# Small reductions over pairs of columns in place of small tensor_scalar operations, the floor of the scales moved into the maxima, and a new table of orders

## The chip, the core and the metric

The kernel runs on one core of one Trainium2 chip. A core has engines that each work through a queue of their own: TensorE (matmuls, which read SBUF and write PSUM), VectorE, ScalarE (both read and write SBUF and PSUM), GpSimd (SBUF only; POOL in the profile) and SyncE (SP), which here only issues DMA transfers. They wait for each other by semaphores. The metric is the device time of one execution in microseconds; lower is better.

## The reference, cut to what matters

A batch of 16 images (3 x 96 x 96) is cut into 36 patches of 16 x 16, each mapped to 256 features; a class token goes in front, 128 text tokens behind: 165 tokens of 256 features per image. On them one transformer layer works:

```python
h = concat([tok(x), txt], axis=1)                     # 16 x 165 x 256
h = h + attn(layernorm(h), Wq, Wk, Wv, Wo)            # 16 heads, 4 key heads, window |q-k| <= 32, rope, softmax
h = h + ffn(layernorm(h), w1, conv_w, conv_b, w2)

def act_quant(x):
    scale = 127.0 / clip(max(abs(x), axis=-1, keepdims=True), 1e-05)
    return clip(round(x * scale), -128, 127) / scale
def weight_quant(w):
    scale = 1.0 / clip(mean(abs(w)), 1e-05)
    return clip(round(w * scale), -1, 1) / scale
def ffn(x, w1, conv_w, conv_b, w2):                   # 256 -> 1024 -> 256
    g = act_quant(x) @ weight_quant(w1).T
    g = silu(depthwise_conv1d(g, conv_w, conv_b))     # three taps along the tokens
    return act_quant(g) @ weight_quant(w2).T
```

What the change touches is the variance of each layernorm (`var + eps`) and, in each `act_quant`, the scale of a token: `max(amax, 1e-05) / 127`, its reciprocal, and its product with the scale of the weights.

## The kernel before

The 16 images are worked in eight pairs (n = 0 to 7) of 330 tokens. A pair's tokens lie as 3 tiles of 110 partitions (t = 0 to 2); attention goes over 11 blocks (j) of 30 queries with a key window of up to 94, in 3 groups (k) of four, four and three blocks; the FFN goes over 8 slices (m) of 128 hidden features in two halves, for the last pair in four quarters. All pairs are in flight as in a pipeline: while the attention of pair n runs, the FFN of pair n-2 or n-1 is between its pieces.

Each piece of work is a small function on its engine that waits for its semaphores and issues its instructions. The order in which an engine takes them is written out by hand in the table ORDER (and ONCE for what happens once): a place in the engine's queue for each piece. Each engine walks the places upwards. An engine never goes past a piece that waits, so a place decides both when a piece may start and what it holds up.

The pieces that the change and the prediction's steps touch, by engine:

- VectorE, startup: sort_pix and keep_pix (L1293, L1298) arrange the pixels of the four image loads; stats1(n) (L1337, L1341, L1344) takes mean and variance of a pair's tokens, after the DMA that moves its patch tokens into `h`; abs_w (L1307, two of them) sums |w1| and |w2|, and ternary (L1314 to L1330) rounds the weights.
- VectorE, attention: max_s(n,j) (L1393) is the row maximum of the scores in PSUM; TensorE's shift(n,j) (L1760) waits for it. norm(n,k) (L1401, L1403) divides by the sums; add_att(n,t) (L1409, L1411) adds the output projection and takes statistics; var2(n) (L1418, L1421) makes the variance, of which GpSimd's rstd2 (L976) makes the power -0.5 and norm2 (L1027) the normalised `xn2` in SBUF.
- VectorE, scale of the FFN input: max_x(n) takes the largest |x| per token (L1428), the clipped scale (L1431), its reciprocal (L1433), for which ScalarE's quant_x (L1174) waits, and the product with the weight scale w1s (L1434), for which GpSimd's dequant_x (L1035) waits. low_x (L1441) splits the input for TensorE's up(n,m) (L1840, L1841).
- FFN: mid on ScalarE (L1190) and taps(n,m) on VectorE (L1449, L1452) make the convolution; tanh on ScalarE (L1198); silu on VectorE (L1458) or on GpSimd (L1043, L1045, two passes over 128 x 1320, both operands in SBUF); abs_g on ScalarE (L1206); max_g on VectorE (L1475, L1479, L1482; for the last pair L1468, L1473). scale_2(n) is max_x's counterpart (L1489, L1492, L1494, L1495); TensorE's spread (L1855) waits for its reciprocal. quant_g (L1502), ScalarE's conv_g (L1213), TensorE's down(n,t) (L1867) and add_ffn(n,t) (L1510) follow. store sends a pair out.
- The last pair's norm is cut by tiles and made on VectorE: var_last(t) (L1516, L1518), rstd_last(t) on GpSimd (L1049), norm_last(t) (L1523 to L1540, seven small or 110 x 256 operations), turn_last(t) on TensorE (L1874), high_last, low_last (L1546), then up(7,m).

Of the kernel before, what the change touches and what calls it, by code (L numbers as in the profile page):

```python
# [103 lines left out]
def tok_tiles(n):  # L104
# [28 lines left out]
        (182, 184),
        (246, 250),
        (328, 334),
        (395, 402),
    ),
    'pe.project': (
        (6, 7, 8),
        (24, 32, 42),  # L140
        (84, 87, 97),
        (136, 141, 147),
        (187, 190, 204),
        (252, 264, 268),
        (339, 343, 347),
        (411, 417, 424),
    ),
    'pe.turn_q': (
        (11, 12, 15),
        (46, 57, 66),  # L150
        (105, 116, 121),
        (154, 169, 174),
        (208, 225, 230),
        (287, 300, 312),
        (360, 371, 384),
        (447, 452, 460),
    ),
    'pe.turn_k': (
        (13, 14),
        (68, 73),  # L160
        (124, None),
        (179, None),
        (239, None),
        (322, None),
        (387, None),
        (485, None),
    ),
# [50 lines left out]
    'pe.select': (
        (49, 71, 90),
        (123, 142, 157),  # L220
        (193, 220, 241),
        (272, 293, 319),
        (344, 368, 389),
        (421, 457, 476),
        (496, 521, 536),
        (564, 589, 600),
    ),
# [1734 lines left out]
```

## Time and profile before

| | before |
|---|---|
| median of 3 runs | 401.66 us (400.25 to 404.05) |
| profiled execution | 399.73 us, of which the span 397.9 us |
| TensorE matmul busy | 343.9 us (86%), 2910 instructions |
| VectorE busy | 302.5 us (76%), 643 |
| ScalarE busy | 259.2 us (65%), 486 |
| GpSimd busy | 248.2 us (62%), 244 |
| chain that ended last | TensorE 49%, VectorE 20%, GpSimd 14%, issue 6%, DMA 5%, ScalarE 4% |
| granted TensorE clock, mean | 0.956 of full speed; lower only near 25 us and in the last 30 us |

The span is the time from the first to the last instruction. Busy shares are means over stages with different limits, so they do not say what bounds the kernel; the busy time by stretch and the waits within a stretch do. A group of instructions has one row with its count, its busy time in all and the mean duration of one. In a timeline, the bracket at the end of a row is the time that the engine stood idle before it, and what it had waited for. The chain that ended last is followed back from the last instruction, at each step to what released it.

### The profile page before, as it was taken

Reading aid. Unit: us, or ns where it says so; the run is one execution under the profiler, and the core shown is the slowest. Engines: PE = TensorE matmul, PEld = TensorE weight load, DVE = VectorE, ACT = ScalarE, POOL = GpSimd, SP = SyncE. Lnnn points to the kernel's source line nnn. Section 1 sums busy time; section 2 is a strip of 40 time slices with the busy share of each in tenths; the row PEclk is TensorE's granted clock in tenths of the full one; section 3 lists DMA queues with packets and bytes.
Section 4 is the critical chain, followed back from the end, with each engine's and each line's share of the span. In section 5 each row is a group of like instructions: output and inputs, shape, how many; then the busy total and the mean of one; then the engine's idle time right before and its main releaser. Section 6 shows DMA issues by size and latency. Waiting matters only on the chain.

```text
span 397.9 us, 8286 instructions
## 1 busy us (share of the span) xinstructions
PE 343.9 (86%) x2910; PEld 267.9 (67%) x2910; DVE 302.5 (76%) x643; ACT 259.2 (65%) x486; POOL 248.2 (62%) x244
## 2 busy tenths in 40 slices
PE   1579999999999989999999997989989989844564
PEld 1356666767787668867986796778857857634454
DVE  2164548744568889897889759998888899898984
ACT  3232554857767869867887767679777787534732
POOL 3407189299899994999489957991760563051510
PEclk9998999999999999999999999999999999995856
DMA  7772161000000100020001002000010210001001
GB/s 233 170 163 55 34 213 28 16 13 15 26 20 18 35 1 3 17 59 20 6 18 33 9 18 61 17 0 2 2 26 22 69 49 1 2 0 36 1 16 52
DMA packets 20250, 15.71 MB, mean 39 GB/s; under 512 B 11035, under 2 KB 19160, under 8 KB 20209
## 3 DMA queue, kind: packets, MB, share of 16 engines
q1 hardware_dynamic: 19314, 14.02, 13.7%
q10 hardware_dynamic: 895, 1.16, 1.1%
q8 instruction: 23, 0.38, 0.4%
q14 instruction: 18, 0.15, 0.1%
HBM read 7.91 MB, written 2.70 MB: 27 GB/s over the span
## 4 chain that ended last, share of the span: by engine, by line
PE 49%; DVE 20%; POOL 14%; issue 6%; DMA 5%; ACT 4%; SPq 1%; ACTq 0%; DVEq 0%; POOLq 0%
PE bank L1769 6%; PE bank L1840 4%; PE bank L1867 4%; PE bank L1784 3%; PE bank L1841 3%; POOL shared L1027 3%; PE bank L1741 3%; PE bank L1689 3%; PE bank L1760 3%; PE bank L1811 3%; DMA cst<-in_consts 3%; PE bank L1636 2%; POOL shared L1035 2%; PE bank L1752 2%; PE bank L1802 2%
## 5 line engine op out<-in xcount | busy, mean ns | idle before, releaser
L1393 DVE TENSOR_REDUCE mx<-bank 120x4 fp32r<-120x376 f32 (+3 forms) x88 | 44.5, 509 | 29.7 <-PE bank L1752 28.9
L1154 ACT COPY pT<-bank 94x480 f32<-94x480 f32 (+3 forms) x88 | 48.6, 555 | 15.4 <-PE bank L1769 14.9
L1145 ACT ACTIVATE pr<-bank 120x376 f32<-120x376 f32 (+3 forms) x88 | 39.9, 457 | 26.0 <-PE bank L1760 25.2
L1769 PE MATMUL bank<-cst,pr 120*94 120x120 f32 (+3 forms) x352 | 51.1, 269 | 3.2 <-ACT pr L1145 2.8
L1840 PE MATMUL bank<-xT_hi,w1T 128*128 128x330 f32 x128 | 45.6, 362 | 4.1 <-DVE wn L1452 2.4
L1769 PEld LDWEIGHTS bank<-cst,pr 120*94 120x94 f32 (+3 forms) x352 | 36.6, 121 | 12.5 <-ACT pr L1145 6.7
L1841 PE MATMUL bank<-xT_lo,w1T 128*128 128x330 f32 x128 | 41.1, 326 | 0.0
L1689 PE MATMUL bank<-wqk,xnT 128*110 128x384 f32 x96 | 36.8, 512 | 0.2
L1760 PE MATMUL bank<-mx,neg_id 120*120 120x376 f32 (+3 forms) x88 | 33.0, 386 | 4.0 <-DVE mx L1393 3.9
L1867 PE MATMUL bank<-w2T,shared 128*110 128x256 bf16 x192 | 29.2, 305 | 8.0 <-DVE h L1510 3.7
L1752 PE MATMUL bank<-kbd,q_hl 128*120 128x376 f32 (+3 forms) x88 | 36.1, 410 | 0.0
L1741 PE MATMUL bank<-kbd,q_hl 128*120 128x376 f32 (+3 forms) x88 | 35.6, 405 | 0.5 <-ACT pT L1154 0.4
L1043 POOL TENSOR_TENSOR shared<-shared,wn 128x1320 f32<-128x1320 f32 (+1 forms) x5 | 12.2, 2436 | 35.0 <-ACT shared L1198 35.0
L983 POOL TENSOR_SCALAR xn<-h,mv,rs 110x256 f32<-110x256 f32 x21 | 27.9, 1336 | 9.6 <-PE bank L1677 9.4
L1784 PE MATMUL bank<-pT,vw 94*32 94x120 f32 (+3 forms) x704 | 33.5, 286 | 0.2
L1867 PEld LDWEIGHTS bank<-w2T,shared 128*110 128x110 bf16 x192 | 24.6, 146 | 10.6 <-issue 5.3
L976 POOL TENSOR_TENSOR rs<-ve,half_neg 110x3 f32<-110x3 f32 x15 | 15.1, 1005 | 25.5 <-DVE ve L1344 18.9
L1027 POOL TENSOR_SCALAR shared<-h,mv,rs 110x256 f32<-110x256 f32 x21 | 30.2, 1449 | 1.1 <-POOL rs L976 1.1
L1840 PEld LDWEIGHTS bank<-xT_hi,w1T 128*128 128x128 f32 x128 | 25.5, 199 | 7.3 <-DVE wn L1452 3.2
L1035 POOL TENSOR_SCALAR shared<-shared,am 110x256 f32<-110x256 f32 x21 | 25.4, 1220 | 6.4 <-ACT shared L1174 6.4
L1005 POOL TENSOR_TENSOR qkr<-rc,rsn 110x160 f32<-110x160 f32 x44 | 26.8, 631 | 1.7
L1784 PEld LDWEIGHTS bank<-pT,vw 94*32 94x32 f32 (+3 forms) x704 | 18.8, 144 | 12.1 <-issue 8.2
(149 smaller groups left out, 918.4 us busy)
## 6 DMA issues: line engine op xcount, KB each, us to landing
out<-h SPq DMA_DIRECT2D x7, 330.0 KB
wn<-in_w SPq DMA_DIRECT2D x2, 1024.0 KB, 7.0
kbd<-kT SPq DMA_DIRECT2D x96, 20.6 KB, 1.9
shared<-in_x SPq DMA_DIRECT2D x4, 432.0 KB
h<-in_txt SPq DMA_DIRECT2D x1, 770.0 KB
wlT<-in_lin SPq DMA_DIRECT2D x1, 768.0 KB, 7.3
h<-tokp SPq DMA_DIRECT2D x14, 36.0 KB
h<-in_txt SPq DMA_DIRECT2D x1, 448.0 KB
```

The source lines that it names most:

```text
L1027: o = nc.gpsimd.tensor_scalar(xn2[:, t, :], h[:, n, t, :], mv2[:, t, 0:1], rs2[:, t:t + 1], ALU.subtract, ALU.mult)
L1154: nc.scalar.copy(pT[0:cnt, g % 3, :], S_BANKS[g % 2][0:cnt, 0:HKV * QP]).then_inc(p_kept, 1)
L1393: nc.vector.tensor_reduce(mx[:, g % 4, :].bitcast(F32R), S_BANKS[g % 2][0:QP, 0:HKV * KEYS[j][1]].rearrange("p (k c) -> p k c", k=HKV), ax ...
L1689: o = nc.tensor.matmul(qk_bank(n, t)[0:TT, 0:QKC + QK], xnT[:, k, t * TT:(t + 1) * TT], wqk[:, k, :], start=(k == 0), stop=(k == KD - 1))
L1741: nc.tensor.matmul(dst, q, kbd[n % 2][:, 0, :, k0:k0 + cnt].bitcast(F32R), start=True, stop=False)
L1752: o = nc.tensor.matmul(dst, q, kbd[n % 2][:, 1, :, k0:k0 + cnt].bitcast(F32R), start=False, stop=True)
L1760: nc.tensor.matmul(S_BANKS[g % 2][0:QP, 0:HKV * cnt], neg_id[:, :].bitcast(F32R), mx[:, g % 4, :].bitcast(F32R).unsqueeze(2).to_broadcast( ...
L1769: o = nc.tensor.transpose(S_BANKS[g % 2][0:cnt, kv * QP:(kv + 1) * QP], pr[:, g % 3, kv * cnt:(kv + 1) * cnt], ident[0:QP, 0:QP])
L1784: o = nc.tensor.matmul(C_BANK[VS * kv:VS * (kv + 1), col:col + QP], vw[n % 2][0:cnt, j, :, kv], pT[0:cnt, g % 3, kv * QP:(kv + 1) * QP], s ...
L1840: nc.tensor.matmul(dst, w, xT_hi[:, k, :].bitcast(F32R), start=(k == 0), stop=False)
L1841: o = nc.tensor.matmul(dst, w, xT_lo[:, k, :].bitcast(F32R), start=False, stop=(k == KD - 1))
L1867: o = nc.tensor.matmul(down_bank(n, t), gq[:, m, t * TT:(t + 1) * TT], w2T[:, m, :], start=(m == 0), stop=(m == MH - 1))
```

## The change

Small operations. In stats1 and var2 the addition of eps to three variances was a tensor_scalar; now the tile `mv` has a third column that holds eps, and a tensor_reduce adds the pair (variance, eps). In max_x and scale_2 a tensor_scalar took the maximum with the floor and multiplied by 1/127, and another multiplied by the weight scale; now new tiles `two1` and `two2` hold pairs (value, 1/127) and (scale, weight scale), and a tensor_reduce multiplies each pair. The floor went elsewhere: for the FFN input it is a 257th column of each row of `xn2` that the maximum takes in; for the hidden activations it is the scalar of a scalar_tensor_tensor that takes the place of the last tensor_tensor maximum of max_g. The constants are written by four VectorE memsets at its start and one GpSimd memset in norm2(0). The last pair's norm_last keeps its tensor_scalar operations; its var_last takes the new form. `xn2` now has rows of 257 columns, so `ga` behind it starts three columns later.

```diff
-        xn2, at = carve(shared, at, TT, [NT, D])
+        xn2, at = carve(shared, at, TT, [NT, D + 1])
...
-        mv1 = sb("mv1", [TT, NT, 2])
+        mv1 = sb("mv1", [TT, NT, 3])
...
+        two1 = sb("two1", [TT, 2, NT, 2])
+        two2 = sb("two2", [TT, 2, NT, 2])
...
+                if n == 0:
+                    nc.gpsimd.memset(xn2[:, :, D:D + 1], CLIP_MIN)
...
+            nc.vector.memset(two1[:, 0, :, 1:2], 1.0 / QMAX)
+            nc.vector.memset(two2[:, 0, :, 1:2], 1.0 / QMAX)
+            nc.vector.memset(mv1[:, :, 2:3], LN_EPS)
+            nc.vector.memset(mv2[:, :, 2:3], LN_EPS).then_inc(guards_made, 1)
...
-                    nc.vector.tensor_scalar(w2s[:, :], wstat[:, 1:2], 0.5, None, ALU.mult)
+                    nc.vector.tensor_scalar(two1[:, 1, :, 1], wstat[0:TT, 0:1].to_broadcast([TT, NT]), 1.0, None, ALU.mult)
+                    nc.vector.tensor_scalar(two2[:, 1, :, 1], wstat[0:TT, 1:2].to_broadcast([TT, NT]), 0.5, None, ALU.mult)
...
-                nc.vector.tensor_scalar(ve2[:, :], mv2[:, :, 1], LN_EPS, None, ALU.add).then_inc(var2, 1)
+                nc.vector.tensor_reduce(ve2[:, :], mv2[:, :, 1:3], axis=AX.X, op=ALU.add).then_inc(var2, 1)
...
-                nc.vector.tensor_reduce(am1[:, 0, :], xn2[:, :, :], axis=AX.X, op=ALU.max,
+                nc.vector.tensor_reduce(two1[:, 0, :, 0], xn2[:, :, :], axis=AX.X, op=ALU.max,
                                         apply_absolute_value=True).then_inc(max1, 1)
                 dve.wait_ge(max1, n + 1)
-                nc.vector.tensor_scalar(am1[:, 1, :], am1[:, 0, :], CLIP_MIN, 1.0 / QMAX, ALU.max, ALU.mult).then_inc(clip1, 1)
+                nc.vector.tensor_reduce(two1[:, 1, :, 0], two1[:, 0, :, :], axis=AX.X, op=ALU.mult).then_inc(clip1, 1)
                 dve.wait_ge(clip1, n + 1)
-                nc.vector.reciprocal(am1[:, 2, :], am1[:, 1, :]).then_inc(scale1, 1)
-                nc.vector.tensor_scalar(am1[:, 3, :], am1[:, 1, :], w1s[0:TT, 0:1], None, ALU.mult).then_inc(undo1, 1)
+                nc.vector.reciprocal(am1[:, 2, :], two1[:, 1, :, 0]).then_inc(scale1, 1)
+                nc.vector.tensor_reduce(am1[:, 3, :], two1[:, 1, :, :], axis=AX.X, op=ALU.mult).then_inc(undo1, 1)
...
-                    nc.vector.tensor_tensor(gm[:, 2, :], gm[:, 0, :], gm[:, 1, :], ALU.max).then_inc(g_maxed, 1)
+                    nc.vector.scalar_tensor_tensor(out=gm[:, 2, :], in0=gm[:, 0, :], scalar=2 * CLIP_MIN, in1=gm[:, 1, :],
+                                                   op0=ALU.max, op1=ALU.max).then_inc(g_maxed, 1)
...
```

stats1, scale_2 and var_last change in the same way.

New orders. Almost every row of ORDER and many of ONCE have new places, on all engines. Two rows as a sample:

```diff
     'pe.turn_xs': (
-        (145,), (205,), (286,), (386,), (433,), (510,), (573,), (None,),
+        (146,), (211,), (299,), (383,), (430,), (515,), (573,), (None,),
     ),
...
-    'dve.norm_last': (284, 293, 300),
-    'dve.var_last': (277, 289, 298),
+    'dve.norm_last': (281, 297, 298),
+    'dve.var_last': (274, 288, 296),
```

VectorE at the first row maxima, before. The rows are keep_k of pair 0 (`kbd`), the first two row maxima (`mx`), stats1(2) (`st`, `mv`, `ve`), four more maxima and the first sum of |w|:

```order
L1384 TENSOR_SCALAR kbd<-bank,cst 128x330 x4
L1393 TENSOR_REDUCE mx<-bank 120x4 x2
L1337 BN_STATS st<-h 110x6 x3
L1341 BN_AGGR mv<-st 110x2 x3
L1344 TENSOR_SCALAR ve<-mv 110x3
L1393 TENSOR_REDUCE mx<-bank 120x4 x4
L1307 TENSOR_REDUCE wabs<-wn 128x1
```

The same place in the changed kernel, in its own line numbers (1396 for 1384, 1405 for 1393, 1347, 1351 and 1356 for 1337, 1341 and 1344, 1316 for 1307):

```order
L1396 TENSOR_SCALAR kbd<-bank,cst 128x330 x4
L1347 BN_STATS st<-h 110x6 x3
L1351 BN_AGGR mv<-st 110x2 x3
L1356 TENSOR_REDUCE ve<-mv 110x3
L1405 TENSOR_REDUCE mx<-bank 120x4 x2
L1347 BN_STATS st<-h 110x6 x3
L1351 BN_AGGR mv<-st 110x2 x3
L1356 TENSOR_REDUCE ve<-mv 110x3
L1405 TENSOR_REDUCE mx<-bank 120x4 x2
L1316 TENSOR_REDUCE wabs<-wn 128x1
L1405 TENSOR_REDUCE mx<-bank 120x4
L1316 TENSOR_REDUCE wabs<-wn 128x1
```

stats1(2) moved ahead of the first two maxima, stats1(3) behind them, and the two sums of |w| stand behind the fourth and the fifth maximum; before they stood behind the sixth and the eighth.

On VectorE in the last pair, before, norm_last(1) stands right behind norm(7,2) (`rcp`, `ctxn`), and taps(6,6) behind it:

```order
L1401 RECIPROCAL rcp<-bank 120x12
L1403 TENSOR_TENSOR ctxn<-bank,rcp 120x192
L1523 TENSOR_SCALAR shared<-h,mv,rs 110x256
L1528 TENSOR_REDUCE am<-shared 110x1
L1531 TENSOR_SCALAR am<-am 110x1
L1534 TENSOR_SCALAR am<-am,w1s 110x1
L1535 RECIPROCAL am<-am 110x1
L1537 TENSOR_SCALAR shared<-shared,am 110x256
L1540 TENSOR_SCALAR shared<-shared,am 110x256
L1449 SCALAR_TENSOR_TENSOR shared<-bank,conv,shared 128x2x164
L1452 SCALAR_TENSOR_TENSOR shared<-bank,conv,shared 128x2x164
```

After, norm_last(1) (L1537 to L1554) comes behind taps(6,7) (L1461, L1464) and var_last(2) (L1530, L1532), and norm_last(2) begins with the last row:

```order
L1461 SCALAR_TENSOR_TENSOR shared<-bank,conv,shared 128x2x164
L1464 SCALAR_TENSOR_TENSOR shared<-bank,conv,shared 128x2x164
L1530 BN_AGGR mv<-st 110x2
L1532 TENSOR_REDUCE ve<-mv 110x1
L1537 TENSOR_SCALAR shared<-h,mv,rs 110x256
L1542 TENSOR_REDUCE am<-shared 110x1
L1545 TENSOR_SCALAR am<-am 110x1
L1548 TENSOR_SCALAR am<-am,w1s 110x1
L1549 RECIPROCAL am<-am 110x1
L1551 TENSOR_SCALAR shared<-shared,am 110x256
L1554 TENSOR_SCALAR shared<-shared,am 110x256
L1537 TENSOR_SCALAR shared<-h,mv,rs 110x256
```

Between norm(7,2) and norm_last(1) now lie taps(6,4) to taps(6,7), add_ffn(5,1) and add_att(7,2). silu(6,1), which stood ahead of norm_last(2), stands behind it. GpSimd's queue at this place is as before: rstd_last(0), rstd_last(1), silu(6,0), rstd_last(2).

## Rows read from the trace of the kernel before

**Rows 1.** Busy time by stretch: engine us (x instructions), PEclk, DMA share, GB/s
```profile
60.00:240.00 180.00, 174.84 (x1617) 137.40 (x1615) 137.81 (x300) 133.43 (x262) 147.93 (x160) 1.00 0.08 20
240.00:340.00 100.00, 91.77 (x851) 72.94 (x849) 91.31 (x178) 76.38 (x136) 58.80 (x44) 1.00 0.10 25
340.00:380.00 40.00, 23.31 (x154) 18.90 (x152) 36.70 (x80) 21.48 (x32) 14.65 (x8) 0.79 0.04 9
380.00:398.00 18.00, 10.04 (x46) 8.27 (x46) 11.05 (x21) 5.79 (x8) 0.00 (x0) 0.59 0.14 38
```

**Rows 2.** Groups by line and shape, VectorE, small operations: busy us, mean ns | idle before
```profile
L1434 DVE TENSOR_SCALAR am<-am,w1s 110x3 f32<-110x3 f32 x7 | 4.6, 659 | 0.0
...
L1495 DVE TENSOR_SCALAR am<-am,w2s 110x3 f32<-110x3 f32 x8 | 2.7, 332 | 0.0
...
L1492 DVE TENSOR_SCALAR am<-am 110x3 f32<-110x3 f32 x8 | 2.5, 310 | 0.3
...
L1421 DVE TENSOR_SCALAR ve<-mv 110x3 f32<-110x3 f32 x7 | 1.8, 253 | 0.2
...
L1431 DVE TENSOR_SCALAR am<-am 110x3 f32<-110x3 f32 x7 | 1.5, 213 | 0.2
...
L1344 DVE TENSOR_SCALAR ve<-mv 110x3 f32<-110x3 f32 x8 | 1.4, 173 | 0.3
```

**Rows 3.** Tile am, whole kernel: xcount, ns fastest/middle/slowest, first and last start, shape
```profile
L1428 DVE TENSOR_REDUCE am<-shared x7: 933/942/953, 102.4 to 325.6; 110x3 f32<-110x768 f32 x7
...
L1434 DVE TENSOR_SCALAR am<-am,w1s x7: 198/201/2780, 103.9 to 326.9; 110x3 f32<-110x3 f32 x7
...
L1528 DVE TENSOR_REDUCE am<-shared x3: 420/420/420, 341.8 to 360.4; 110x1 f32<-110x256 f32 x3
...
L1537 DVE TENSOR_SCALAR shared<-shared,am x3: 354/355/2053, 342.8 to 361.4; 110x256 f32<-110x256 f32 x3
```

**Rows 4.** Timeline near 244 us: start us, us, engine, line [idle before <- releaser]
```profile
244.42 2.98 POOL L1043 TENSOR_TENSOR shared<-shared,wn 128x1320 f32<-128x1320 f32 x1 [2.44 <-ACT shared L1198]
...
244.64 2.78 DVE L1434 TENSOR_SCALAR am<-am,w1s 110x3 f32<-110x3 f32 x1
...
247.95 1.05 PE L1867 MATMUL bank<-w2T,shared 128*110 128x256 bf16 x8 [2.07 <-DVE h L1510]
```

**Rows 5.** Chain that ended last, near 147 us: start us, us, what
```profile
147.48 0.78 DVE am L1492
```

**Rows 6.** Groups by line and shape, VectorE and GpSimd, more durations
```profile
L1307 DVE TENSOR_REDUCE wabs<-wn 128x1 f32<-128x2048 f32 x2 | 4.6, 2276 | 0.0
...
L1468 DVE TENSOR_TENSOR shared<-shared 128x330 f32<-128x330 f32 x4 | 2.0, 497 | 0.3 <-ACT shared L1206 0.3
...
L960 POOL MEMSET half_neg<- 110x3 f32 x1 | 0.1, 102 | 0.3 <-POOLq L1931 0.3
```

**Rows 7.** Timeline of VectorE, then GpSimd, in the last pair
```profile
345.51 0.56 DVE L1452 SCALAR_TENSOR_TENSOR shared<-bank,conv,shared 128x328 f32<-128x328 f32 x1
...
349.89 1.16 DVE L1523 TENSOR_SCALAR shared<-h,mv,rs 110x256 f32<-110x256 f32 x1
...
352.04 2.05 DVE L1537 TENSOR_SCALAR shared<-shared,am 110x256 f32<-110x256 f32 x1
...
359.95 0.41 DVE L1523 TENSOR_SCALAR shared<-h,mv,rs 110x256 f32<-110x256 f32 x1 [0.44 <-POOL rs L1049]
...
347.88 3.02 POOL L1043 TENSOR_TENSOR shared<-shared 128x1320 f32<-128x1320 f32 x1
...
350.97 2.97 POOL L1045 TENSOR_TENSOR shared<-shared 128x1320 f32<-128x1320 f32 x1
```

**Rows 8.** Timeline of VectorE at the first row maxima
```profile
46.87 1.00 DVE L1393 TENSOR_REDUCE mx<-bank 120x4 fp32r<-120x264 f32 x2 [2.20 <-PE bank L1752]
...
49.20 1.08 DVE L1337 BATCH_NORM_STATS2 st<-h 110x6 f32<-110x256 f32 x3 [1.33 <-DMA h<-tokp]
...
50.66 0.17 DVE L1344 TENSOR_SCALAR ve<-mv 110x3 f32<-110x3 f32 x1
```

More of the change, by code:

```diff
@@ L129 @@
         (3, 4),
-        (19, 21),
-        (78, 80),
+        (17, 19),
+        (73, 78),
         (128, 131),
[L133 to L136, printed above, removed]
+        (183, 186),
+        (248, 250),
+        (328, 332),
+        (406, 419),
     ),
     'pe.project': (
[L139 to L146, printed above, removed]
+        (5, 6, 8),
@@ L147 @@
+        (22, 25, 30),
+        (81, 86, 91),
+        (136, 142, 145),
+        (189, 193, 200),
+        (253, 260, 277),
+        (339, 345, 350),
+        (422, 428, 433),
     ),
     'pe.turn_q': (
[L149 to L156, printed above, removed]
+        (11, 13, 16),
+        (40, 46, 55),
+        (104, 107, 118),
+        (154, 171, 173),
@@ L157 @@
+        (207, 225, 231),
+        (284, 297, 309),
+        (362, 371, 392),
+        (443, 467, 476),
     ),
     'pe.turn_k': (
[L159 to L166, printed above, removed]
+        (14, 15),
+        (56, 62),
+        (122, None),
+        (181, None),
+        (240, None),
+        (320, None),
+        (396, None),
+        (487, None),
     ),
     'pe.scores': (
[8 rows of a table removed]
[8 rows of a table added]
@@ L217 @@
     ),
     'pe.select': (
[L219 to L226, printed above, removed]
+        (48, 74, 93),
+        (119, 141, 157),
+        (190, 213, 242),
+        (276, 294, 318),
+        (346, 368, 387),
+        (421, 451, 481),
+        (496, 516, 538),
+        (562, 584, 599),
     ),
     'pe.out_proj': (
-        (54, 74, 94),
-        (127, 144, 167),
@@ L262 @@
-        (533, 542, 554),
-        (581, 592, 601),
+        (237, 243, 255),
+        (300, 312, 323),
+        (379, 394, 409),
+        (469, 475, 492),
+        (526, 531, 546),
+        (585, 598, 604),
         (616, 617, 618),
@@ L469 @@
         (92, 95),
[L470 removed]
+        (125, 129),
         (163, 167),
[L472 to L475 removed]
+        (205, 211),
+        (240, 242),
+        (276, 277),
+        (310, 311),
         (None, None),
@@ L1034, in dequant_x @@
                 for t in range(NT):
-                    o = nc.gpsimd.tensor_scalar(xn2[:, t, :], xn2[:, t, :], MAGIC, am1[:, 3, t:t + 1],
+                    o = nc.gpsimd.tensor_scalar(xn2[:, t, 0:D], xn2[:, t, 0:D], MAGIC, am1[:, 3, t:t + 1],
                                                 ALU.subtract, ALU.mult)
@@ L1340, in stats1_of @@
                 for t in range(NT):
-                    o = nc.vector.bn_aggr(mv1[:, t, :], st1[:, t, :])
+                    o = nc.vector.bn_aggr(mv1[:, t, 0:2], st1[:, t, :])
                 o.then_inc(aggr1, 1)
                 dve.wait_ge(aggr1, n + 1)
-                nc.vector.tensor_scalar(ve1[:, :], mv1[:, :, 1], LN_EPS, None, ALU.add).then_inc(var1, 1)
+                if n == 0:
+                    dve.wait_ge(guards_made, 1)
+                nc.vector.tensor_reduce(ve1[:, :], mv1[:, :, 1:3], axis=AX.X, op=ALU.add).then_inc(var1, 1)
             def norm1(n):
@@ L1472, in max_g @@
                             dve.wait_ge(g_maxed, n + p - 1)
-                        nc.vector.tensor_tensor(gm[:, 2, :], gm[:, 2, :], gm[:, part, :], ALU.max).then_inc(g_maxed, 1)
+                        nc.vector.scalar_tensor_tensor(out=gm[:, 2, :], in0=gm[:, 2, :], scalar=2 * CLIP_MIN, in1=gm[:, part, :],
+                                                       op0=ALU.max, op1=ALU.max).then_inc(g_maxed, 1)
                     return
@@ L1515, in var_last @@
                 dve.wait_ge(xn2_made, PAIRS - 1)
-                nc.vector.bn_aggr(mv2[:, t, :], st2[:, t, :]).then_inc(last_aggr, 1)
+                nc.vector.bn_aggr(mv2[:, t, 0:2], st2[:, t, :]).then_inc(last_aggr, 1)
                 dve.wait_ge(last_aggr, t + 1)
-                nc.vector.tensor_scalar(ve2[:, t:t + 1], mv2[:, t, 1:2], LN_EPS, None, ALU.add).then_inc(last_var, 1)
+                nc.vector.tensor_reduce(ve2[:, t:t + 1], mv2[:, t, 1:3], axis=AX.X, op=ALU.add).then_inc(last_var, 1)
             def norm_last(t):
@@ L1522, in norm_last @@
                 dve.wait_ge(xs_turned, PAIRS - 1)
-                nc.vector.tensor_scalar(xn2[:, t, :], h[:, PAIRS - 1, t, :], mv2[:, t, 0:1], rs2[:, t:t + 1],
+                nc.vector.tensor_scalar(xn2[:, t, 0:D], h[:, PAIRS - 1, t, :], mv2[:, t, 0:1], rs2[:, t:t + 1],
                                         ALU.subtract, ALU.mult).then_inc(last_normed, 1)
@@ L1527, in norm_last @@
                 dve.wait_ge(xs_made, PAIRS - 1)
-                nc.vector.tensor_reduce(am1[:, 0, t:t + 1], xn2[:, t, :], axis=AX.X, op=ALU.max,
+                nc.vector.tensor_reduce(am1[:, 0, t:t + 1], xn2[:, t, 0:D], axis=AX.X, op=ALU.max,
                                         apply_absolute_value=True).then_inc(last_max, 1)
```

322 lines of the change are left out of this document (158 added, 164 removed), and 160 rows, old and new, of the table ORDER.

## The prediction

> **What bounds the kernel now.** I read the busy time by stretch first [rows 1]. From 60 to 240 us TensorE is busy 174.8 of 180 us at full clock: little but its own work decides there. From 240 to 340 us TensorE (91.8) and VectorE (91.3) are both above nine tenths. From 340 to 380 us VectorE is busy 36.7 of 40 us and TensorE 23.3: the last pair's FFN waits for VectorE, and an operation held there moves the end. The last 18 us are a chain in which all take turns.
>
> Then the small VectorE operations, by shape [rows 2]. They read three numbers per partition, yet line 1434 takes 659 ns in the mean, 1495 332, 1492 310, 1421 253. The spread explains it [rows 3]: line 1434 has a fastest and a middle near 0.20 us and a slowest of 2.78. The timeline at 244 us shows the slowest [rows 4]: GpSimd's 2.98 us multiply over 1,320 columns starts at 244.42, the small operation at 244.64, and both end at 247.4. TensorE's down projection waited 2.07 us for the addition queued behind it. So a small tensor_scalar with SBUF operands is held while GpSimd works. A tensor_reduce out of SBUF is not: line 1428 stands three places ahead of 1434 and has 933/942/953 ns [rows 3].
>
> **The small operations.** They are 7 + 8 + 8 + 7 + 7 + 8 = 45, busy 4.6 + 2.7 + 2.5 + 1.8 + 1.5 + 1.4 = 14.5 us [rows 2]. The price of the new form: no row shows a reduction over pairs, but 768 columns take 942 ns and 256 take 420 [rows 3], so 1.02 ns a column on a base of 159; six columns make about 0.165 us. Below, it could hardly be under the base (0.159); above, the nearest row itself is 0.42. I take 0.165, since both rows give the line. 45 x 0.165 = 7.4 us, so VectorE loses 7.1 us of work; at 0.42 it would be 18.9, so 4.4 more than now. The three single-tile variances of the last pair change by nothing to speak of.
>
> Of these 7.1 us only what someone waited for counts:
> - The stall at 244 us: 2.78 - 0.20 = 2.6 us on VectorE, 2.07 of it waited for by the matmuls [rows 4], with both engines above nine tenths. I take 2.1.
> - The other stalls: 4.6 - 7 x 0.2, 2.7 - 8 x 0.2, 2.5 - 8 x 0.17, 1.8 - 7 x 0.17 and 1.5 - 7 x 0.17 make 6.4 us; less 2.6 leaves 3.8. Most lie before 240 us, under a TensorE that idles 3%. The chain of the end runs through one of them, 0.78 us at 147 us for an operation that takes 0.17 undisturbed [rows 5], so 0.6 of it counts; of the 3.2 others I take a fifth. Together 1.2, between 0 and 3.8.
>
> The Trainium skill has a rule for this, page "SBUF — State Buffer", section "Who interferes with whom": VectorE and GpSimd share a second port pair as an exclusive lock; tensor_scalar from SBUF to SBUF can take it, tensor_reduce never does, and an operation with two SBUF inputs contends with a GpSimd that reads. The rows agree for the first two (2.78 against 0.94 us). By it all 6.4 us of stalls go. Against the change stands the page "VectorE: DVE Perf Modes", section "Rules for kernel authors": tensor_reduce is "the slowest DVE op", to be kept off a hot path. The two reduction rows do not show it for six columns; what it would make of the time is among the rivals.
>
> **The other edits.** The floor in the maxima turns 10 tensor_tensor of 330 columns into scalar_tensor_tensor: 497 ns for the old form [rows 6], 0.56 us for 328 columns of the new with a PSUM input [rows 7]. At most 10 x 0.06 = 0.6 us; I take nothing, both read the same two tensors. The four VectorE memsets run before the identity matrix has landed, when the engine has nothing else; uncovered they cost 0.1 each, like GpSimd's small one [rows 6]. One such memset goes in front of norm2 of pair 0 on GpSimd: 0.1 us. The padded rows of xn2 (257 columns) add 3 columns, 3 ns, to line 1428. Whether the odd pitch costs other engines no row shows; I hold 0 to 0.7 us (a tenth of seven such reductions) and take nothing.
>
> **The new order at the end of the kernel.** Before, norm_last(1) starts at 349.89 on VectorE, just after GpSimd began its silu of pair 6 (347.88 to 353.94): its first pass takes 1.16 us where the one at 359.95 takes 0.41, its fourth 2.05 where the middle is 0.355 [rows 3, 7]. That is 0.75 + 1.70 = 2.45 us in a stretch that VectorE bounds, and these operations stay tensor_scalar. Then silu(6,1) stands ahead of norm_last(2), which still waits 0.44 us for its rstd [rows 7]. In the new order norm_last(1) and (2) stand side by side behind taps(6,7) and var_last(2). The last tap of taps(6,3) ends at 346.07; it lets ScalarE's tanh and then GpSimd's silu go, done 7.9 us later. Between it and norm_last(1) VectorE now has eight taps of 0.56, 4.5 us, and by my estimate from their neighbours some 3 us of additions, statistics and one normalisation: 7.5 us, so the two meet for 0.4 us. The rstd of norm_last(2) is made under norm_last(1). The gain is 2.45 + 0.44 - 0.4 = 2.5; I take 2.4. If GpSimd is still at it, up to 2.45 stays.
>
> **The new order at the start.** Here I see a cost. stats1(2) waits for patch tokens that land at 49.20 us; the variance behind it ends at 50.83 [rows 8]. Before, the first two row maxima of pair 0 stand ahead of it, from 46.87, 0.5 us each. Now stats1(2) stands ahead of them. What lets the tokens go (SP's queue, the patch product before) is not moved, so the first maximum ends near 51.3 in place of 47.4: 4.0 us later, and TensorE's shift(0,0) with it. Between scores(0,0) and shift(0,0) TensorE has only half of turn_xn(1), so I take two thirds of the 4.0, 2.7 us, as new TensorE idleness. GpSimd's rstd for pair 2 comes no later than before (it hung on the same tokens), so not all is passed on: I take half, 1.4 us, between 0 and 4. From 60 to 340 us most items move by a few places; I see neither a term nor a sign, and hold 2 us either way.
>
> **Sum.** 2.1 + 1.2 + 2.4 - 1.4 = 4.3 us. The profiled execution took 399.73 us (span 397.9 and 1.8 around it), so it would come to 395.4. The median of the runs is 401.66, 1.9 above it; I carry the difference over: 401.66 - 4.3 = 397.4 us.
>
> **The rivals.**
> - The gain is larger: TensorE's spare work covers the start (0 lost), half of the other stalls counts (1.9), and the middle gives 1.5: 2.1 + 1.9 + 2.4 + 1.5 = 7.9, 393.8 us. For it: VectorE's nine tenths from 240 us on. Against: TensorE's 97% before. Chance 0.20.
> - Nothing to tell: the start takes what the stalls give: 2.1 + 0 + 1.2 - 3 = 0.3, 401.4 us. For it: before 240 us TensorE hardly waits, so what VectorE saves there nobody waited for. Chance 0.20.
> - The reductions are slow: 0.42 us each, 0.255 more than in my sum, 11.5 us in all; of the 45 some 18 come after 240 us, and their 4.6 us are passed on: 401.66 - 4.3 + 4.6 = 402.0. Against: the line through the two reduction rows. Chance 0.05. It is the case in which the second page's rule holds.
> - Slower, by one mechanism: pair 0's attention is held on VectorE. Behind the late first maximum come stats1(3) (1.6 us, as stats1(2)) and, earlier among the maxima than before, the two sums of |w|, 2.28 us each [rows 6]. If TensorE's spare work covers none of it, 4.0 + 1.6 + 4.6 = 10.2 us are passed on against 5.7 of gain: 401.66 + 4.5 = 406.2. It decides from 9.7 passed on. Against: TensorE has project(1) and turn_q(1) to do meanwhile. Chance 0.13.
> - My forecast, 394.5 to 399.5 us: 0.42.
>
> **How the numbers follow.** About 1% (4 us) is what a measurement of this kernel can tell from no change: faster is below 397.6, slower above 405.7. Of the forecast's 0.42 I put 0.27 below 397.6; with the larger gain 0.47. The slower case and 0.01 of the others give 0.14; 0.39 remain. The range 391.5 to 404.5 leaves out about 0.05 on the fast side and 0.15 on the slow one. The forecast's own range is 394.5 to 399.5.
>
> **What would show it.** Right: the lines in place of 1421, 1431, 1434, 1492 and 1495 have means of 0.16 to 0.18 us and no slow one; VectorE's busy total falls by about 7 us for them and 2 for norm_last; the 2 us wait near 245 us is gone; stats1(2) waits for tokens ahead of the first maximum, which ends at 50 to 52 us. Wrong: small reductions near 0.3 us or with slow ones; other operations held in their stead (the maxima with two SBUF inputs, norm_last); a stretch from 340 us to the end as long as now; or a first maximum at 47 us, by which my cost at the start falls and the larger gain is due.

## The result, and the profile after

Twenty runs of each kernel, in turn on one chip: 402.76 us before (399.29 to 409.47), 404.56 after (402.36 to 407.17). Both are medians of all 20; six runs of before fell in a slower state that some executions show and are left out of the ratio, which is therefore higher than that of the two medians. The ratio is 1.0073, with a 95% interval of 1.0045 to 1.0101. The change makes the kernel 0.7% slower, 2.9 us, where I had forecast 4.3 us less. That is within the 1% band that I had called no change, but on the other side of it. The profiled execution took 402.36 us (span 400.4; before 399.73 and 397.9); it is the fastest of the 20, so its rows show the loss at its mildest.

From the page of the changed kernel, its busy time and its chain that ended last (shares of the span):

```profile
PE 347.4 (87%) x2910; PEld 270.3 (68%) x2910; DVE 292.2 (73%) x648; ACT 259.3 (65%) x486; POOL 245.9 (61%) x245
...
PE 57%; POOL 12%; DVE 8%; issue 8%; ACT 6%; DMA 4%; SPq 3%; ACTq 0%; POOLq 0%; DVEq 0%
```

VectorE was busy 302.5 us before and is now busy 292.2. The saving came as forecast, and the kernel is slower all the same. TensorE, 343.9 before, went up to 347.4 for the same 2,910 products. Some of them run at a lower clock, as the windows 45 to 50 and 50 to 55 us show, before and then after (behind the busy times stands PEclk, the granted clock):

```profile
45.00:50.00 5.00, 4.63 (x26) 3.16 (x26) 1.78 (x5) 1.98 (x5) 0.00 (x0) 1.00 0.21 55
50.00:55.00 5.00, 4.62 (x31) 2.92 (x30) 1.86 (x7) 2.29 (x6) 3.92 (x6) 1.00 1.01 374
```
```profile
45.00:50.00 5.00, 2.88 (x13) 2.44 (x14) 3.50 (x12) 3.44 (x9) 1.02 (x2) 0.63 0.62 187
50.00:55.00 5.00, 5.00 (x15) 2.77 (x15) 1.88 (x7) 1.41 (x4) 4.84 (x5) 0.69 0.64 247
```

The small operations, by tile and by line (times in ns: fastest, middle, slowest), answer to [rows 2, 3]:

```profile
L1506 DVE TENSOR_REDUCE two<-two x8: 159/159/160, 150.4 to 388.8; 110x3 f32<-110x6 f32 x8
...
L1509 DVE TENSOR_REDUCE am<-two x8: 128/129/131, 150.7 to 389.1; 110x3 f32<-110x6 f32 x8
L1440 DVE TENSOR_REDUCE two<-shared x7: 947/949/959, 104.6 to 330.2; 110x3 f32<-110x771 f32 x7
L1443 DVE TENSOR_REDUCE two<-two x7: 159/159/160, 105.6 to 331.2; 110x3 f32<-110x6 f32 x7
...
L1356 DVE TENSOR_REDUCE ve<-mv x8: 158/159/161, 23.4 to 195.8; 110x3 f32<-110x6 f32 x8
```

None is slow any more: slowest 161 ns, where line 1434 before had 2,780. Busy time by stretch, as in [rows 1]:

```profile
60.00:240.00 180.00, 172.36 (x1598) 133.54 (x1597) 130.49 (x284) 131.81 (x258) 143.33 (x156) 1.00 0.09 21
240.00:340.00 100.00, 93.47 (x862) 75.22 (x860) 85.78 (x182) 75.78 (x139) 60.39 (x47) 1.00 0.09 22
340.00:380.00 40.00, 26.97 (x181) 22.06 (x182) 37.24 (x85) 25.39 (x40) 13.49 (x8) 0.84 0.04 10
380.00:410.00 30.00, 12.45 (x54) 10.09 (x52) 12.29 (x24) 6.27 (x9) 0.00 (x0) 0.68 0.08 23
```

From 60 to 240 us TensorE does 1,598 products where it did 1,617; from 340 us on it has 235 to do where it had 200. By 60 us it had already done 30 fewer (220 for 250). The kernel is behind by 240 us, and it never gets back what it lost. The start, VectorE and then TensorE (start us, us, [idle before <- releaser]), answers to [rows 8]:

```profile
47.09 1.08 DVE L1347 BATCH_NORM_STATS2 st<-h 110x6 f32<-110x256 f32 x3 [0.48 <-DMA h<-tokp]
...
48.63 0.42 DVE L1405 TENSOR_REDUCE mx<-bank 120x4 fp32r<-120x264 f32 x1
...
53.63 1.08 DVE L1347 BATCH_NORM_STATS2 st<-h 110x6 f32<-110x256 f32 x3 [2.55 <-POOL xn L986]
...
56.08 0.55 DVE L1405 TENSOR_REDUCE mx<-bank 120x4 fp32r<-120x376 f32 x1 [0.83 <-PE bank L1766]
```
```profile
47.12 0.78 PE L1691 MATMUL bank<-cst,xn 110*128 110x110 f32 x3 [2.14 <-ACT q_hl L1128]
```

The first maximum (L1405) stands behind stats1(2) (L1347), and the third behind stats1(3), which itself waits for GpSimd's norm1(2) (L986). TensorE's pause of 2.14 us lies ahead of the first scores: it waits for ScalarE to copy the turned queries (L1128), and patches(3), which before stood between the last turn_q and the scores and filled that time, now stands ahead of turn_q(0,1). In this execution TensorE waits neither for the first maximum nor for the third.

### The profile page after: what moved, and what is told of

Its sections match the earlier page's. It is cut to its first block, busy times and chain, and to the rows that moved or that the text cites. A ratio compares the mean times of both kernels' runs of the same rounds, so it can differ in the third digit from the quotient of the medians.

```text
span 400.4 us, 8293 instructions
## 1 busy us (share of the span) xinstructions
PE 347.4 (87%) x2910; PEld 270.3 (68%) x2910; DVE 292.2 (73%) x648; ACT 259.3 (65%) x486; POOL 245.9 (61%) x245
## 4 chain that ended last, share of the span: by engine, by line
PE 57%; POOL 12%; DVE 8%; issue 8%; ACT 6%; DMA 4%; SPq 3%; ACTq 0%; POOLq 0%; DVEq 0%
PE bank L1783 6%; PE bank L1703 6%; PE bank L1798 5%; PE bank L1881 4%; PE bank L1854 4%; PE bank L1755 4%; PE bank L1855 3%; PE bank L1825 3%; PE bank L1650 3%; SPq L925 3%; PE bank L1774 3%; DMA cst<-in_consts 3%; PE bank L1766 2%; PE bank L1816 2%; POOL shared L1048 2%
## 5 line engine op out<-in xcount | busy, mean ns | idle before, releaser
L1405 DVE TENSOR_REDUCE mx<-bank 120x4 fp32r<-120x376 f32 (+3 forms) x88 | 44.8, 511 | 31.4 <-PE bank L1766 30.3
L1783 PEld LDWEIGHTS bank<-cst,pr 120*94 120x94 f32 (+3 forms) x352 | 36.4, 121 | 14.5 <-ACT pr L1150 10.1
L1703 PE MATMUL bank<-wqk,xnT 128*110 128x384 f32 x96 | 36.9, 509 | 1.9 <-ACT xnT L1115 1.1
L986 POOL TENSOR_SCALAR xn<-h,mv,rs 110x256 f32<-110x256 f32 x21 | 28.6, 1371 | 14.6 <-PE bank L1691 14.2
L1774 PE MATMUL bank<-mx,neg_id 120*120 120x376 f32 (+3 forms) x88 | 36.2, 414 | 1.1 <-DVE mx L1405 1.0
L1798 PE MATMUL bank<-pT,vw 94*32 94x120 f32 (+3 forms) x704 | 34.9, 288 | 0.7 <-ACT pT L1159 0.6
L1881 PE MATMUL bank<-w2T,shared 128*110 128x256 bf16 x192 | 30.8, 317 | 4.3 <-ACT shared L1238 2.1
L1881 PEld LDWEIGHTS bank<-w2T,shared 128*110 128x110 bf16 x192 | 26.2, 152 | 6.7 <-issue 2.7
L1032 POOL TENSOR_SCALAR shared<-h,mv,rs 110x256 f32<-110x256 f32 x21 | 29.1, 1395 | 1.1 <-POOL rs L979 1.1
L1798 PEld LDWEIGHTS bank<-pT,vw 94*32 94x32 f32 (+3 forms) x704 | 18.9, 145 | 14.5 <-issue 9.2
L1040 POOL TENSOR_SCALAR shared<-shared,am 110x256 f32<-110x256 f32 x21 | 24.5, 1178 | 6.4 <-ACT shared L1179 6.4
```

The lines of the kernel that those rows point to most:

```text
L1405: nc.vector.tensor_reduce(mx[:, g % 4, :].bitcast(F32R), S_BANKS[g % 2][0:QP, 0:HKV * KEYS[j][1]].rearrange("p (k c) -> p k c", k=HKV), ax ...
L1703: o = nc.tensor.matmul(qk_bank(n, t)[0:TT, 0:QKC + QK], xnT[:, k, t * TT:(t + 1) * TT], wqk[:, k, :], start=(k == 0), stop=(k == KD - 1))
L1774: nc.tensor.matmul(S_BANKS[g % 2][0:QP, 0:HKV * cnt], neg_id[:, :].bitcast(F32R), mx[:, g % 4, :].bitcast(F32R).unsqueeze(2).to_broadcast( ...
L1783: o = nc.tensor.transpose(S_BANKS[g % 2][0:cnt, kv * QP:(kv + 1) * QP], pr[:, g % 3, kv * cnt:(kv + 1) * cnt], ident[0:QP, 0:QP])
L1798: o = nc.tensor.matmul(C_BANK[VS * kv:VS * (kv + 1), col:col + QP], vw[n % 2][0:cnt, j, :, kv], pT[0:cnt, g % 3, kv * QP:(kv + 1) * QP], s ...
L1881: o = nc.tensor.matmul(down_bank(n, t), gq[:, m, t * TT:(t + 1) * TT], w2T[:, m, :], start=(m == 0), stop=(m == MH - 1))
```

## The experiments

Ratios are to runs of before on the same chip, with 95% intervals; 1% is 4.0 us. A range behind a difference between two kernels is my estimate from their two intervals. In most of these kernels only the tables of places differ. "The order of before up to T" means: each engine first does, in the order of before, all that it had begun by T us of the trace, and then the rest in the order of after. Where the tables were written with one row per line, line numbers of a kernel are shifted; the prose then says which line of after is meant.

**Operations and orders apart.** e1 has the tables of before and all other edits of the diff; e2 has the tables of after in the old code.

> The new small operations alone, with every engine in the order of before. Theory A (the operations gain what the sum said, 3.3 us for the stalls at small operations, and the new orders then cost about 5): 399.5 us, ratio to before 0.992. Rival B (the stalls on VectorE at small operations only sat where TensorE had other work, so the operations are worth nothing and the 0.7% are the orders' alone): 402.5 us, ratio 0.999 to 1.001. Either way the eight gate reductions and the others take about 160 ns each and no small operation stands for 2 us.

> The new orders alone, with the small operations of before. Theory A: slower than before by the 1.8 us measured for the whole change plus the 3.3 us that the operations gave, 408 us, ratio 1.013. Rival B: as slow as the whole change, 404.6 us, ratio 1.005.

e1: 0.9956 (0.9918 to 0.9995). e2: 1.0222 (1.0169 to 1.0274). In direction theory A holds: the operations gain, and the orders lose more than they gain. Its sizes, 0.992 and 1.013, don't: the first is at the edge of the interval and the second outside it. And the two effects don't add up. The operations are worth 0.4% in the old orders and 1.5% (0.9 to 2.1) in the new ones (1.0222 to 1.0073). The timeline of e2 near 255 us shows the difference; L1564 and L1567 are lines 1431 and 1434 of before, L1973 the up product:

```profile
255.01 2.23 DVE L1564 TENSOR_SCALAR am<-am 110x3 f32<-110x3 f32 x1
257.37 2.92 DVE L1567 TENSOR_SCALAR am<-am,w1s 110x3 f32<-110x3 f32 x1
...
261.79 0.64 PE L1973 MATMUL bank<-xT_hi,w1T 128*128 128x330 f32 x1 [4.27 <-DVE wn L1585]
```

Here two operations in a row are held, 5.2 us, and TensorE waits 4.27. In the order of before one was held there, and TensorE waited 2.07 [rows 4]. What an operation that can be held costs depends on where the order puts it against GpSimd; the new ones take 128 to 161 ns wherever they stand.

**Start and rest apart.** Both have the new operations. e3 is the order of before up to 77 us. e4 is the reverse: the order of after up to 78 us, the order of before behind it.

> The new operations; every engine in the order of before for what it had begun by 77 us of the trace (pair 0's attention nearly done), in the order of after behind that. Theory S (the start carries the loss: VectorE waits for tokens ahead of the first row maxima, TensorE idles and its granted clock falls to 0.83 for 40 to 60 us): near the operations alone, 400 us, ratio 0.993. Theory M (the loss comes between 100 and 240 us, where the trace of after falls from 1 us late to 4 us late): as the whole change, 404 us or little below, ratio 1.00 to 1.005. Half and half gives 402.

> The new operations; every engine in the order of after for what it had begun by 78 us, in the order of before behind that. Theory S: 403 to 404 us, ratio 1.002, slower than the operations alone by 3 to 4. Theory M: as the operations alone or at most 1 us slower, 400 us. The granted clock of 40 to 60 us is 0.83 here and 1.00 in the kernel with the old start, by both.

e3: 0.9966 (0.9928 to 1.0003). e4: 1.0044 (1.0000 to 1.0088). With the new start the kernel is slower by 1.07% (e3 to after, 4.3 us, 2.4 to 6.2) and by 0.88% (e1 to e4, 3.5 us, 1.2 to 5.9), so theory S has its cost. But it is not the whole loss: the new order behind 77 us costs too (the middle, below).

e4 shows what TensorE waits for in the new start. The pause for the turned queries is there again (L1261, line 1128 of after), and then a shorter one for the first maximum, which stands behind the tokens:

```profile
48.58 0.47 PE L1824 MATMUL bank<-cst,xn 110*128 110x110 f32 x3 [2.14 <-ACT q_hl L1261]
...
51.12 0.58 PE L1907 MATMUL bank<-mx,neg_id 120*120 120x264 f32 x1 [1.04 <-DVE mx L1538]
```

The granted clock is 0.54 from 50 to 55 us of e4 and 0.77 from 55 to 60.

**The end.** f4 is the order of before up to 300 us and that of after behind it, norm_last's new place with it.

> The new operations; every engine in the order of before for what it had begun by 300 us of the trace, in the order of after behind that, so that norm_last is placed as after. If my term of 2.4 us for the end stood, 2.4 us less than the operations alone: 398.1 us, ratio 0.990. Rival (the end is bounded by TensorE's up and down products at the low granted clock, and the two held operations of norm_last only waited in its shadow, or they went with the small operations already): as the operations alone, ratio 0.9956, within 0.002.

f4: 0.9894 (0.9854 to 0.9934), 2.5 us less than e1 (0.3 to 4.7). My term of 2.4 us stood, though other places behind 300 us changed with norm_last's and share in the 2.5. The passes of norm_last (lines 1537 and 1551 of after), grouped by line, first in e1, then in f4 (busy us, mean ns | idle before):

```profile
L1684 DVE TENSOR_SCALAR shared<-shared,am 110x256 f32<-110x256 f32 x3 | 2.8, 925 | 0.1
...
L1670 DVE TENSOR_SCALAR shared<-h,mv,rs 110x256 f32<-110x256 f32 x3 | 2.0, 651 | 0.4 <-POOL rs L1187 0.4
```
```profile
L1537 DVE TENSOR_SCALAR shared<-h,mv,rs 110x256 f32<-110x256 f32 x3 | 1.2, 409 | 0.0
...
L1551 DVE TENSOR_SCALAR shared<-shared,am 110x256 f32<-110x256 f32 x3 | 1.1, 355 | 0.1
```

The new operations alone leave norm_last as slow as it was (921 and 659 ns at lines 1537 and 1523 of before); its new place does away with it.

**The middle.** g3 and g4 are the order of before up to 150 and 240 us.

> The new operations; every engine in the order of before for what it had begun by 150 us of the trace, in the order of after behind that. The whole of 77 to 300 us in the new order costs 0.7% (0.9966 with the new order from 77 us, 0.9894 with it from 300 us). If that is lost in 77 to 150 us: ratio 0.990. If it is lost behind 150 us, where the traces part between the first scores of pair 3 (0.8 us apart) and of pair 5 (6.2 us): ratio 0.9966.

> The same with the order of before up to 240 us. If the middle's loss is made in 150 to 240 us: ratio 0.990, as with the new order from 300 us. If it is made in 240 to 300 us: 0.9966.

g3: 0.9927 (0.9895 to 0.9959). g4: 0.9846 (0.9799 to 0.9892). Neither point that I had named holds alone. Read as a row of switch points (77, 150, 240, 300 us: 0.9966, 0.9927, 0.9846, 0.9894), the new order loses 1.6 us from 77 to 150, loses 3.3 from 150 to 240, and gains 1.9 from 240 to 300; only the middle one of these is outside what two intervals allow. TensorE and the other engines from 150 to 240 us, g4 and then g3:

```profile
150.00:240.00 90.00, 89.06 (x845) 72.88 (x847) 74.28 (x158) 70.46 (x134) 71.71 (x70) 1.00 0.09 21
```
```profile
150.00:240.00 90.00, 86.82 (x809) 69.36 (x808) 71.64 (x148) 67.61 (x128) 68.72 (x67) 1.00 0.09 23
```

In the new order TensorE idles 3.2 us there instead of 0.9. The largest piece, in the timeline of g3; the changed kernel has the same 2.73 us:

```profile
171.21 0.48 ACT L1122 COPY qk<-bank 110x384 f32<-110x384 f32 x1 [2.73 <-DMA vw<-qk]
171.59 0.49 ACT L1150 ACTIVATE pr<-bank 120x376 f32<-120x376 f32 x1
...
172.13 0.62 PE L1783 MATMUL bank<-cst,pr 120*94 120x120 f32 x4 [1.80 <-ACT pr L1150]
```

keep_qk (L1122) may not overwrite qk before the transfers of load_v have read it. In the order of before it waits 0.71 us, in the new one 2.73, and an exponential for which TensorE waits stands behind it. This is read from traces; no run tried that step alone.

g4 is the best version: 395.72 us, 1.1 to 2.0% faster than before.

**Single parts put back in the changed kernel.** f1 moves the row statistics of pairs 2 and 3 behind pair 0's maxima and GpSimd's norm1(2) behind rope(1,0). f2 moves patches(3) on TensorE. f3 is the order of before up to 50 us. Of f1 and f2, as they stand in the tables:

```
 'dve.stats1':  - (2,), (7,), (12,), (15,), ...    + (2,), (7,), (14,), (22,), ...
 'pe.patches':  - (1, 9, 10, 12)                   + (1, 9, 10, 16)
```

> The changed kernel with one thing put back on VectorE: stats1(2) stands behind the second maximum of pair 0 and stats1(3) behind norm(0,0), as before, and GpSimd turns rope(1,0) ahead of norm1(2) again. Theory V (row maxima held by waits for tokens and for GpSimd's normalised rows make the start late): 402.0 us, 2.5 to 3 us faster than the changed kernel, ratio to before 1.000; the first row maximum and the third come 1.5 and 3 us earlier. Theory P (TensorE reaches the first scores late because patches(3) stands ahead of the turns of q and k): no more than 0.5 us faster, ratio 1.006.

> The changed kernel with one thing put back on TensorE: patches(3), 3.4 us of products, stands behind turn_q(0,2) instead of ahead of turn_q(0,1). Theory P: 402 us, ratio to before 1.000; the 2.1 us of idle TensorE ahead of the first scores are gone and the clock stays full in 40 to 60 us. Theory V: within 0.5 us of the changed kernel, ratio 1.006, since VectorE's first maximum still waits for the tokens at 47 us and the third for GpSimd.

> The new operations; every engine in the order of before only for what it had begun by 50 us of the trace (15 steps of VectorE, 25 of TensorE), and in the order of after behind that. If the loss is made before 50 us (V and P together): as with the old order up to 77 us, ratio 0.997, 401 us. If it is made between 50 and 77 us (the sums of absolute weights, 2.28 us each on VectorE, between pair 0's maxima, and pair 1's projections ahead of pair 0's maxima): as the changed kernel, ratio 1.005.

f1: 1.0152 (1.0108 to 1.0195), slower than the changed kernel at 1.0073. f2: 1.0054 (1.0020 to 1.0088). f3: 1.0135 (1.0085 to 1.0185), worse than either value that I had named. Theories V and P both fall in the form in which I wrote them: no part gives back the loss. The traces say why. In f1 the first maxima no longer wait for tokens, but norm1(2), itself later now, stands ahead of rope(1,1) on GpSimd, and turn_q(1,1) waits for that. In f2 the scores are early and the first maximum waits for tokens. In f3 the third maximum waits for GpSimd. One line of each:

```profile
66.78 0.60 PE L1716 MATMUL bank<-cst,qsp 110*128 110x110 f32 x4 [3.53 <-POOL qsp L1022]
```
```profile
51.19 0.58 PE L1774 MATMUL bank<-mx,neg_id 120*120 120x264 f32 x1 [3.52 <-DVE mx L1405]
```
```profile
58.65 0.67 PE L1774 MATMUL bank<-mx,neg_id 120*120 120x376 f32 x1 [3.62 <-DVE mx L1405]
```

**The ropes first.** g1 moves pair 1's three rope tiles on GpSimd ahead of rstd1 and norm1 of pair 2, with the maxima free; g2 adds patches(3).

> The changed kernel; the row statistics of pair 2 stand behind pair 0's second maximum on VectorE, and GpSimd does pair 1's three rope tiles (4.8 us each) before it takes pair 2's rstd1 and norm1 (4.5 us), with stats1(3) behind max_s(1,0). Theory G (one chain, tokens to stats1(2) to norm1(2) on GpSimd to rope(1,*) to turn_q(1,*), reaches TensorE's early turns late; moving maxima or products alone only passes the wait on): the waits of 2.2 us for the third maximum and of 3.5 us for turn_q(1,1) seen with the maxima first are both gone; 401 us, 3 to 4 us faster than the changed kernel, ratio to before 0.997. Rival (pair 1's turns are late for another reason, or the early sums of weights cost it): as the changed kernel, ratio 1.007.

> The same with patches(3) behind turn_q(0,2) on TensorE as before. Theory G with P: another 1 us for the idle 2.1 us ahead of the first scores, ratio 0.995. If the patches' place is worth nothing once the maxima are free: as the kernel without this edit, within 0.002.

g1: 1.0120 (1.0069 to 1.0170). g2: 1.0075 (1.0046 to 1.0105). Of theory G the first half held: the wait for turn_q(1,1) is gone and pair 1's first scores start at 76.5 us, in the changed kernel at 79.2, though the third maximum still waits 2.21 us. Then it failed: norm1(2) is now late itself, and TensorE pays at pair 2's turn (g1):

```profile
94.66 1.00 PE L1716 MATMUL bank<-cst,qsp 110*128 110x110 f32 x4 [2.92 <-POOL qsp L1022]
```

**Single parts added to the best kernel.** Undoing single parts only handed the wait on, so I turned it round: g4, whose start is the old one, and one part of the new start in it.

```
 'dve.stats1', h1:  - (4,), (8,), (14,), (22,), ...   + (4,), (8,), (12,), (22,), ...
 'dve.abs_w',  h3:  - (19, 24)                        + (17, 19)
```

> The new operations, the order of before up to 240 us and of after behind it (0.9846), with one edit: VectorE does the row statistics of pair 2, which wait for tokens, ahead of the first row maximum. If my term had its mechanism right (the first maximum goes from 47.7 to about 51.3 us) and only its share was too small: 3.4 us late in pair 0, 2 to 3.5 us at the end, ratio to before 0.990 to 0.993. If the cost of the new start lies elsewhere: under 1 us, ratio 0.985 to 0.987.

> The same, with stats1(3) also ahead of pair 0's third maximum and GpSimd's norm1(2) ahead of rope(1,0), so that the third maximum waits for 3.6 us of GpSimd too. If the two waits add up: another 3 us late in pair 0, 5 to 6 us at the end, ratio 0.998 to 1.000, more than the whole new start costs (0.0107), since pair 1's work does not fill TensorE here as it does in the new order. If the second wait is covered by the first: as with the first alone.

> The kernel with the order of before up to 240 us and one edit: the two sums of absolute weights, 2.28 us each, stand behind pair 0's maxima 3 and 4, as in the changed kernel, instead of 5 and 7. If they hold pair 0's maxima, as my slower rival had it: 1 to 3 us, ratio 0.987 to 0.992. If TensorE has other work meanwhile: within 0.002 of 0.9846.

h1: 0.9968 (0.9939 to 0.9997). h2: 0.9966 (0.9938 to 0.9995). h3: 0.9946 (0.9908 to 0.9983). Against g4's 0.9846 the tokens ahead of the first maximum cost 1.2%, 4.9 us (2.7 to 7.1), where I had given them 2 to 3.5; the second wait costs nothing more. The early sums cost 1.0%, 4.0 us (1.6 to 6.4), where I had given 1 to 3. h1 first (its windows from 45 us with PEclk behind the busy times), then the same two windows of g4:

```profile
48.48 1.08 DVE L1347 BATCH_NORM_STATS2 st<-h 110x6 f32<-110x256 f32 x3 [4.26 <-DMA h<-tokp]
...
50.01 0.87 DVE L1405 TENSOR_REDUCE mx<-bank 120x4 fp32r<-120x264 f32 x2
```
```profile
50.49 0.58 PE L1774 MATMUL bank<-mx,neg_id 120*120 120x264 f32 x1 [3.37 <-DVE mx L1405]
...
52.53 2.77 PE L1703 MATMUL bank<-wqk,xnT 128*110 128x384 f32 x4
```
```profile
45.00:50.00 5.00, 2.13 (x12) 1.40 (x11) 1.46 (x7) 0.43 (x1) 0.00 (x0) 0.90 0.38 102
50.00:60.00 10.00, 9.12 (x41) 6.23 (x42) 1.98 (x5) 4.14 (x10) 4.73 (x8) 0.71 0.50 181
```
```profile
45.00:50.00 5.00, 4.63 (x27) 3.28 (x26) 1.84 (x6) 2.02 (x6) 0.00 (x0) 1.00 0.22 62
50.00:60.00 10.00, 9.61 (x76) 6.33 (x75) 4.61 (x10) 5.75 (x13) 8.84 (x12) 1.00 0.58 205
```

TensorE idles 3.37 us, and then its granted clock is 0.71 over the ten us in which it has to make up. It is as busy as in g4 (9.1 and 9.6 us) and does 41 products instead of 76. The four products of L1703 take 2.77 us; at full clock, in g4 at 49.51 us, they take 1.54. h1's first scores start 0.85 us ahead of g4's; by scores(0,5) of pair 0 the lag is 4.6 us, by pair 1's first scores still 4.6, and at the end of the profiled spans 6.2. In h3 the same happens ten us later, on another transfer (windows of h3 behind the lines of VectorE and TensorE):

```profile
56.91 2.29 DVE L1316 TENSOR_REDUCE wabs<-wn 128x1 f32<-128x2048 f32 x1 [2.56 <-DMA wn<-in_w]
```
```profile
59.64 0.39 PE L1774 MATMUL bank<-mx,neg_id 120*120 120x312 f32 x1 [1.63 <-DVE mx L1405]
...
62.29 0.67 PE L1774 MATMUL bank<-mx,neg_id 120*120 120x376 f32 x1 [1.12 <-DVE mx L1405]
```
```profile
60.00:70.00 10.00, 8.88 (x75) 6.30 (x74) 4.70 (x11) 4.20 (x9) 7.68 (x12) 0.66 0.04 9
```

h1 and h3 price one part in g4, where it meets other neighbours than in the changed kernel. There the first sum begins without a wait, its weights having landed, and TensorE waits for neither maximum behind the sums:

```profile
57.44 2.28 DVE L1316 TENSOR_REDUCE wabs<-wn 128x1 f32<-128x2048 f32 x1
```

## Why the prediction was right or wrong

- **Price of the reductions, 0.165 us: right**, 159 ns for the sums and for half of the products, 129 for the other half (L1446, L1509). VectorE's 45 operations went from 14.5 to 6.7 us, 7.8 less against 7.1. The rival of slow reductions is out. The Trainium skill, page "VectorE: DVE Perf Modes", section "Rules for kernel authors", calls tensor_reduce "the slowest DVE op": for six columns the trace disagrees, at 159 ns against 201 for the middle one of line 1434's undisturbed tensor_scalars [rows 3]. The other edits, taken at nothing, show next to none: norm2, which writes the rows of odd pitch, is busy 29.1 us on GpSimd for 30.2, and the maximum over the padded rows takes 949 ns for 942.
- **Stalls at 244 us and elsewhere, 2.1 + 1.2: mechanism right, size high.** The stalls are gone; e1 measures 1.8 us for it (0.2 to 3.3), and my 3.3 is the upper end of that. In e1 pair 6's first scores are 4.3 us earlier in the profile than before (263.25 against 267.54), pair 7's first 2.7 earlier and its last only 0.3 (336.48 against 336.78). So most is lost again ahead of norm_last. From 320 to 340 us the granted clock is 0.83 in e1's profile and 1.00 before; these are two single executions, and no run tried what takes the rest.
- **The end, 2.4: right**, measured at 2.5 (e1 to f4, 0.3 to 4.7).
- **The start, -1.4: this step failed.** "GpSimd's rstd for pair 2 comes no later than before [...], so not all is passed on: I take half, 1.4 us, between 0 and 4." The whole new start measures 4.3 us (2.4 to 6.2; e3 to after) and 3.5 (e1 to e4). One half of the mechanism was there: with tokens landing at 49.1 us (e4) the first maximum ends at 51.06, where I had said 51.3. Three things in the term were wrong. First, the waits: I put 2.7 us of new TensorE idleness behind the first maximum, and there are 1.04 in e4 and none in the changed kernel's profile. The longer pause, 2.14 us in both, is the one for the turned queries, from the new place of patches(3), which I had not looked at. The two stand in a row, and so f2, which takes the first away, leaves 3.52 us for the second. Second, I counted on half being given back. In h1, where the tokens are the only change, 4.6 us of lag at pair 1 come out as 4.9 (2.7 to 7.1) at the end: TensorE has about 97% of its time filled from 60 to 240 us, which I had read myself in [rows 1]. Third, I priced the wait as idle time only, and left out the clock behind it, 0.63 from 45 to 50 us and 0.69 from 50 to 55 in the changed kernel. How the 4.3 us split between idle time, clock and the rest of the new places is not shown.
- **The sums of |w|** had a price only in the slower rival, 4.6 us. h3 measures 4.0, but 2.56 us of VectorE's time there is a wait for weights that the changed kernel's profile doesn't have, so this is not their price in the change. stats1(3) ahead of the third maximum, in that rival at 1.6, costs nothing on top of the tokens (h2). The whole new start, 3.5 to 4.3 us, is well below that rival's 10.2; that its waits overlap and that the early project(1) fills some of TensorE's time would fit, but no run shows it.
- **The middle, no term, 2 us either way: wrong.** It costs 2.9 us net from 77 to 300 us (e3 to f4, 0.7 to 5.1): 4.8 are lost ahead of 240 and 1.9 come back behind it.

Summed: -1.8 - 2.5 + 2.9 + 4.3 = +2.9 us. These are steps from before over e1, f4 and e3 to after, so they must end at the measured 0.73%; the sum is no check. Of my forecast the gains came in at 4.3 for 5.7, the losses at 7.2 for 1.4. On the prediction's base the result is 401.66 + 2.9 = 404.6 us, a little above the top of my range, 404.5. By its number it lies nearest to the slower rival (406.2), by class with "nothing to tell" (within 1%). The latter's sentence, that the start takes what the stalls give, is true as far as it goes; what the orders cost in the middle stands in no rival. Open is whether there is a loss between 77 and 150 us (1.6 us, within the intervals) and its cause, and how much of the 3.3 behind it is the wait for load_v.

## What to carry to other kernels

Where an engine is 97% filled for the next 180 us, a wait ahead of that stretch can be passed on whole, as in h1; ask about slack behind the wait, not at it, and add the slower clock that follows the idle time. When an operation that waits for a transfer is moved forward on its engine, list what stands behind it there and who waits for that. Work that fills a wait, as patches(3) did ahead of the first scores, opens that wait when it is moved. And measure code and order apart: here the small operations and the orders from 240 us on gave 1.5% together, and the table of places that came with them took more than that away.
